# A fused transformer sandwich on one core: weighted sums in two pieces, the first batch's splits on other engines, later loads issued later

## The reference

```python
c_kv = x @ W_kv_down
k_rope = _rotary_apply(c_kv @ W_k_rope, cos, sin)
k = (c_kv @ W_k_up).reshape(Bb, Tt, NH, HD)          # NH = 16 heads, HD = 16
v = (c_kv @ W_v_up).reshape(Bb, Tt, NH, HD)
q = (x @ W_q).reshape(Bb, Tt, NH, HD)
q_rope = _rotary_apply(x @ W_q_rope, cos, sin)
scores = jnp.einsum('bqhd,bkhd->bhqk', q, k)
scores = scores + jnp.einsum('bqr,bkr->bqk', q_rope, k_rope)[:, None]
scores = scores / math.sqrt(HD + D_R)
scores = jnp.where(causal[None, None], -jnp.inf, scores)
w = jax.nn.softmax(scores, axis=-1)
attn = jnp.einsum('bhqk,bkhd->bqhd', w, v).reshape(Bb, Tt, D_MODEL)
return attn @ W_o
```

## Time and profile before

| | |
|---|---|
| median of 3 runs | 1363.53 us (1363.21 to 1367.56) |
| the profiled execution | 1369.83 us, span 1368.0 us |
| PE busy | 1197.1 us, 88% |
| DVE busy | 1114.6 us, 81% |
| ACT busy | 1057.5 us, 77% |
| POOL busy | 258.2 us, 19% |
| mean granted TensorE clock | 0.945 |
| weighted sums on PE (L982) | 2560 records, 93.3 us busy |
| turns of the weights on PE (L964) | 1280 records, 201.0 us busy |
| copies of the turned weights on ACT (L1217) | 300, 172.1 us busy |

### The profile page before, as it was taken

One profiled execution on the slowest core, in us unless ns is written; L12 is line 12 of the kernel. 1 busy time (PEld: TensorE's weight loads), 2 busy tenths in 40 slices (PEclk: granted clock), 3 DMA queues, 4 the chain that ended last, 5 costly groups with the idle time before them and its releaser, 6 DMA issues.

```text
span 1368.0 us, 23221 instructions
## 1 busy us (share of the span) xinstructions
PE 1197.1 (88%) x8060; PEld 774.9 (57%) x8060; DVE 1114.6 (81%) x2323; ACT 1057.5 (77%) x2113; POOL 258.2 (19%) x253
## 2 busy tenths in 40 slices
PE   5898985989899899998899999999999998973867
PEld 2574754466555655665655755676565764641434
DVE  3693588898689988999899998899889997799930
ACT  4675799768979989798868989698968987548542
POOL 3952001300121103200131010400131111111011
PEclk9799997999999999999999999999899998995979
DMA  8412350424134115311452131612342131013000
GB/s 256 107 23 73 59 147 26 111 44 126 40 80 98 24 47 159 85 30 32 134 121 57 25 103 46 147 23 59 107 106 58 24 119 39 31 56 100 16 16 16
DMA packets 72083, 101.64 MB, mean 74 GB/s; under 512 B 10640, under 2 KB 44064, under 8 KB 71968
## 3 DMA queue, kind: packets, MB, share of 16 engines
q1 hardware_dynamic: 71968, 100.16, 27.9%
HBM read 74.44 MB, written 25.69 MB: 73 GB/s over the span
## 4 chain that ended last, share of the span: by engine, by line
PE 51%; ACT 20%; DVE 17%; issue 8%; DMA 2%; POOL 1%; SPq 0%; POOLq 0%; DVEq 0%; ACTq 0%
PE ps L881 21%; PE ps L890 13%; DVE work L1526 6%; ACT work L1210 4%; PE ps L964 4%; PE ps L982 3%; DVE work L1445 3%; ACT work L1217 3%; ACT xnd L1153 3%; PE ps L956 3%; PE ps L1050 2%; DVE work L1535 1%; PE ps L873 1%; DVE work L1400 1%; ACT work L1276 1%
## 5 line engine op out<-in xcount | busy, mean ns | idle before, releaser
L1526 DVE TENSOR_TENSOR_SCAN work<-work 128x512 f32<-128x512 f32 x256 | 305.3, 1223 | 31.1 <-ACT work L1276 29.1
L1210 ACT ACTIVATE work<-work 128x384 f32<-128x384 f32 (+3 forms) x512 | 265.8, 564 | 42.5 <-DVE work L1445 41.6
L763 POOL TENSOR_TENSOR later_norms<-later_norms,singles 128x2 f32<-128x2 f32 x112 | 101.6, 910 | 884.0 <-ACT xnd L1153 577.0
L1445 DVE CUSTOM_DVE_ANT_0 work<-ps,work 128x384 f32<-128x384 f32 (+3 forms) x512 | 224.2, 485 | 48.1 <-PE ps L956 44.9
L964 PE MATMUL ps<-ident,work 128*128 128x128 f32 x1280 | 201.0, 282 | 25.0 <-ACT work L1210 23.2
L964 PEld LDWEIGHTS ps<-ident,work 128*128 128x128 f32 x1280 | 151.4, 145 | 75.2 <-issue 52.1
L1217 ACT COPY work<-ps 128x512 f32<-128x512 f32 x300 | 172.1, 579 | 3.9 <-PE ps L964 3.7
L1535 DVE TENSOR_TENSOR work<-work 128x1024 f32<-128x1024 f32 x128 | 161.9, 1265 | 5.1
L956 PE MATMUL ps<-work 96*128 96x384 bf16 (+3 forms) x512 | 123.7, 310 | 10.6 <-DMA work<-scratch 5.2
L881 PE MATMUL ps<-led_xTd,wf 128*128 128x512 f32 x256 | 124.7, 635 | 6.7 <-issue 6.0
L890 PE MATMUL ps<-wf,hid 128*128 128x256 f32 x512 | 116.9, 389 | 4.4 <-ACT hid L1292 3.6
(11 more groups left out here) (177 smaller groups left out, 1919.6 us busy)
## 6 DMA issues: line engine op xcount, KB each, us to landing
work<-values SPq DMA_DIRECT2D x64, 256.0 KB, 3.2
work<-ratios SPq DMA_DIRECT2D x64, 256.0 KB, 3.3
scratch<-work SPq DMA_DIRECT2D x32, 384.0 KB, 4.8
work<-scratch SPq DMA_DIRECT2D x64, 192.0 KB, 3.9
work<-scratch SPq DMA_DIRECT2D x64, 128.0 KB, 4.2
x_in<-x SPq DMA_DIRECT2D x8, 512.0 KB, 6.5
work<-scratch SPq DMA_DIRECT2D x64, 64.0 KB, 4.2
values<-work SPq DMA_DIRECT2D x16, 256.0 KB, 2.7
```

The costliest lines, as they stand in the source:

```text
L763: g_.tensor_tensor(rstds[chain][:, tokens], spreads[chain][:, tokens], power[:, tokens], ALU.pow).then_inc(*rstd.one)
L1210: i = s_.activation(part_of, part_of, ACT.Exp, scale=-1.0, bias=nmax[:, row:row + 1])
L1445: i = v_.tensor_tensor_reduce(sc[:, n % 4, at:at + nk], out_of(b, name)[:, at:at + nk], base_of(qt), -SCORE_SCALE, BIG, ALU.add, ALU.min, ...
L1526: v_.tensor_tensor_scan(ring[:, at, m, :], pwr[:, slot, :], ring[:, at, m, :], 0.0, ALU.mult, ALU.add).then_inc(*scanned.one)
```

## The change

The second and the third piece of a group's weighted sums become one. The list of items keeps the lag of five units, so a group has a piece after units 3 and 9, of 32 and 48 records. Units 4 to 7 are thus held in their slots until the last piece. In batch 0 a new item "cast" has ACT cast the rest and DVE subtract, in place of POOL. The twelve later loads go to a function that SP calls in batch 0 after the load of group 1. `MERGE` and `BANKS` are new for all engines.

```diff
-SUMS = ((3,), (2, 0), (1,))
-SUM_OF = (0, 0, 0, 0, 1, 1, 1, 1, 2, 2)
-SUM_AFTER = (3, 7, 9)
+SUMS = ((3,), (2, 0, 1))
+SUM_OF = (0, 0, 0, 0, 1, 1, 1, 1, 1, 1)
+SUM_AFTER = (3, 9)
...
-    items = ["ckv", ("q", 0), ("q", 1), ("pieces", 0), "qr", ("k", 0), ("k", 1), ("pieces", 1), "kr", ("v", 0), ("v", 1),
+    items = ["ckv", ("q", 0), ("cast", 0), ("q", 1), ("cast", 1), ("pieces", 0), "qr", ("k", 0), ("cast", 2), ("k", 1), ("cast", 3),
+             ("pieces", 1), "kr", ("v", 0), ("v", 1),
...
+            def load_rest():
+                load(raw_re, w_in_re)
...
+                load(b2r[:], b2)
...
                     load_group(b, n)
+                    if b == 0 and n == 1:
+                        load_rest()
...
-                if item in ("q", "k"):
+                if item in ("q", "k") and b:
...
-                    need_given(pool, second_piece)
+                    need(pool, second_piece, b, n + 1 + DC * (item == "k"))
...
-                    for m in range(last - 1 if k == 2 else last - 3, last + 1):
+                    for m in range(hg * UNITS + (SUM_AFTER[k - 1] + 1 if k else 0), last + 1):
...
+                if item == "cast" and b == 0:
+                    name, piece = (f"k{n - DC}", k_pieces[:, n - DC, 1, :]) if n >= DC else (f"q{n}", q_pieces[:, n, 1, :])
+                    is_drained(act, b, name)
+                    s_.copy(piece, rest[:, n % DC, :]).then_inc(*second_piece.one)
...
+                if item == "cast" and b == 0:
+                    pieces, pick = (q_pieces, (1, 2)) if n < DC else (k_pieces, (1, 0))
+                    need(dve, second_piece, b, n + 1)
+                    v_.tensor_tensor(pieces[:, n % DC, pick[1], :], rest[:, n % DC, :], pieces[:, n % DC, pick[0], :],
+                                     ALU.subtract).then_inc(*third_piece.one)
```

More of the change, by code:

```diff
@@ L164 @@
     "pe": "xT ckv q qr k kr v base S T PV OT attnT out fxT fc fproj zxT z total query gather oout gxT gc gproj prep",
-    "act": "ystats fstats fystats zstats oystats gstats gystats centre norm xT q k v S T PV attnT fnorm fxT fc znorm zxT z weights query turn fold cos sin silu gnorm gxT gc gsum ternary prep",
-    "dve": "stats ckv q qr k kr base S T OT sum fc fsum z weights ratio total rates turn frac scan mix gate silu "
+    "act": "ystats fstats fystats zstats oystats gstats gystats centre norm xT q cast k v S T PV attnT fnorm fxT fc znorm zxT z weights query turn fold cos sin silu gnorm gxT gc gsum ternary prep",
+    "dve": "stats ckv q cast qr k kr base S T OT sum fc fsum z weights ratio total rates turn frac scan mix gate silu "
            "osum gystats ternary prep tables means late",
@@ L174 @@
     "pe":
[9 rows of a table removed]
-    "act":
[14 rows of a table removed]
-    "dve":
[13 rows of a table removed]
[10 rows of a table added]
+    "act":
[15 rows of a table added]
+    "dve":
[13 rows of a table added]
     "pool":
-        "a2 p a3 p4 a4 d2 a3 d7 a4 d2 a3 d8 a4 d2 a3 d8 a d3 a d a5 d10 a d4 a6 d10 a d4 a3 d2 a3 d9 a d3 a6 d14 "
+        "a p5 a9 d2 a2 d7 a4 d2 a3 d8 a4 d2 a3 d8 a d2 a d a2 d a3 d10 a d4 a6 d12 a d2 a3 d2 a3 d8 a d4 a6 d14 "
         "a2 d26 p4",
     "sp":
-        "a14 d3 m4 d m4 d m9 a6 d2 a m4 d3 m10 a5 m d m2 d a2 d3 m4 d2 m9 a5 m2 d m2 d a2 d3 m4 d m4 d m5 a3 m a2 "
-        "m3 d2 a2 d2 m4 d2 m2 d m9 a3 m a2 m d2 a2 d3 m4 d m5 d m5 a5 m2 d m d a2 d3 m4 d m4 d m8 d m d3 m4 d3 "
-        "m13 d4",
+        "a14 d2 m4 d3 m13 a6 d4 m8 a d m6 a2 m a2 m a d m d a2 d3 m8 d2 m5 a5 m3 d m d a2 d2 m4 d2 m4 d m5 a3 m "
+        "a2 m2 d m d a2 d3 m3 d m5 d m6 a m a2 m a m a d2 a2 d2 m4 d2 m4 d m6 a2 m a3 m2 d2 a2 d2 m4 d3 m13 d5 m8 "
+        "d2 m9 d4",
@@ L229 @@
-3057613054762130547630215476305274163052741630542163054635321403765410642504136205436104275316471256
-4157261750623716520753012752073157235163720561326372406137024561374537025370621475036217241750267502
-4130567412564273015231706253716231540716520462745206742657014271064214710245172035470157263140652316
-7346521730517462305167240516705162405716240573425321067451046145304261534605421730652714637256473256
-4357042364507560276250763125703624135067215473507214536074574261305742613507261350267350216340572163
@@ L234 @@
-4507123013675210372607514306712546170256172065137305216372130710235170423150726140375624705647123056
-413702564137256413072564132056432170564317052643170526431705
+0123450123450134250134250314203512405241024512045320145203420352043251042531025412504125014325140321
+4351234051230541236705412367054123670541236754261375240356472365743025461725364213451046120356471023
+6547130267406342670146032574163702416350241356024135062731406273106542731062437104265732531326735132
+7543743256731463243701426734120746573201456215702456017426315670216403721675640356213547021354217503
@@ new lines @@
+4175203471526340156423654356535637015743176025137016234763127640216705164720531425170315047130651453
+6502163502714635027143560271437561403275614027561402756210453726413762346075340265742360157362045607
+5214720425107234105274307520472542043765124735604172305471302654371243605712436057214367021436702143
+6720451367041652370162756736012534017542073415073104357041732013427105347031765304751364052317064530
+4251634205716305427105632710275106325710634572016534706231057214051026475120637146530173421073524705
@@ L236 @@
+4372650426351472654215762401725643075124630174236701453702614325670143256701325670312670354267512704
+3615024657102674510652073156247035074653763074356145136041501340574153450724157364015237165237401652
+703164527031452703614527034652374016523701652437016524370165
 """
@@ L656, in load_group @@
                     at += k * HD
+            def load_rest():
+                load(raw_re, w_in_re)
+                load(raw_im, w_in_im)
+                load(fac, factors)
+                load(dist, c_dist)
+                load(sel[:], c_sel)
+                load(carry[:], c_carry)
+                load(wz[:], w_in_val)
+                load(wzs[:], w_in_dec)
+                load(wout[:], w_out)
+                load(wf1[:], w1.rearrange("(c p) n -> p c n", p=P))
+                load(wf2[:], w2.rearrange("(c p) n -> p c n", p=P))
+                load(b2r[:], b2)
             load_x(0)
@@ L679, in _ @@
             raw(raw_v[0:RANK], v)
-            load(raw_re, w_in_re)
-            load(raw_im, w_in_im)
-            load(fac, factors)
-            load(dist, c_dist)
-            load(sel[:], c_sel)
-            load(carry[:], c_carry)
-            load(wz[:], w_in_val)
-            load(wzs[:], w_in_dec)
-            load(wout[:], w_out)
-            load(wf1[:], w1.rearrange("(c p) n -> p c n", p=P))
-            load(wf2[:], w2.rearrange("(c p) n -> p c n", p=P))
-            load(b2r[:], b2)
             def do(b, item, n):
```

5 lines of the change are left out of this document (removed), and 74 rows, old and new, of the table MERGE.

## The result

The changed kernel takes 1374.69 us (median of 10 runs, 1369.29 to 1376.82), the kernel before 1364.04 in the same session (ten runs too, one of them at 2056.49, which the median passes over): a ratio of 1.0072, 95% interval 1.0059 to 1.0086. It is slower by some 10 us, where 3 us less had been forecast; the range ended at 1372. A second set of runs gave 1375.07 and 1.0076 (1.0056 to 1.0096).

What follows compares the result with a forecast made beforehand. PE was taken to set the pace in the middle, the first score's delay to pass on in the first batch. Start 3.3 plus tail 0.6 less pieces 7.0 gave −3.1: median 1360.4 us, range 1351 to 1372.

Steps and rivals of the forecast that it cites:

- the pieces' gain: Weighted sums in two pieces: 5.8 us of saved entries and 5.7 of PE waits, 10.8 at most; two thirds taken, 7.0.
- The new wait: ACT's copy of unit 10 waits for the joined piece: 0.05 us a group, counted as nothing, upper end 1.5 a group.
- rival (b): Copy of unit 10 does wait, ACT's exponentials slip, PE waits three units later: +11.9, 1375.4 us; chance 0.13.
- Rival (a): Pieces gain nothing, since ACT and DVE set the pace and PE's freed time idles: +3.9, 1367.4 us; chance 0.17.
- The start: First batch, splits by ACT and DVE: first score 4.0 us later, at 49.1; first batch ends 3.3 later.
- rival (d): POOL's ternary work, slowed by DVE's subtractions, holds DVE at prep 4 until 50.1: 0.8 over forecast, 1361.2 us; chance 0.08.
- Loads put off: Twelve later weight loads moved behind the second group's load: cost nothing, 2 us if the margin is gone.
- The tail: Copy of query 2 ahead of ACT's turns and one addition ahead of the last product: 0.6 us lost (0 to 1.2).
- Past the first batch the lists keep their neighbours: Rewritten lists of all engines keep the same neighbours within a few units past the first batch.
- seams: Other places where the rewritten lists differ: 3 us either way in the range, nothing in the sum.

Runs made afterwards that it cites:

- p2: Kernel before with its own orders, first batch and splits; only the middle piece of the sums joined with the last: 1385.28 us, ratio 1.0152.
- ml_hold: mid_last_c with one wait more: the middle piece also waits for the copies of units 8 and 9; 1377.62 us, ratio 1.0097.
- ml_release: mid_last_c with one wait longer: copies of units 10 to 13 wait for the last piece, not the middle one; 1370.99 us, ratio 1.0055.
- after_ml: Changed kernel with the joined piece split in two again, the middle one directly ahead of the last at the same place: 1369.15 us, ratio 1.0035.
- mid_last_c: Kernel before, three pieces, the middle one moved directly ahead of the last in all 32 groups, nothing else moved: 1366.41 us, ratio 1.0014.
- a3: Changed kernel, its first batch and orders, with three pieces, the middle one back behind the transposes of unit 9: 1402.16 us, ratio 1.0269.
- x_ahead: Kernel before's orders and three pieces behind the changed kernel's first batch, loads put off included: 1369.32 us, ratio 1.0038.
- mid_last: Kernel before, middle piece moved directly ahead of the last in the chain's list, which also shifted other items on PE and ACT: 1401.84 us.
- mid_next_c: Kernel before, three pieces, PE's middle piece one score and one set of transposes later in groups 0 to 2, nothing else moved: 1366.08 us, ratio 1.0005.
- p2_early_c: p2 with the joined piece and ACT's copy of its sums one score and one set of transposes earlier in groups 0 to 2: 1402.76 us, ratio 1.0274.

## Why the prediction was wrong

Two steps failed: the wait that was put at 0.05 us a group and so at nothing, and the two thirds of the pieces' gain that were counted as time.

**The new wait** was 0 in the sum and costs 5 to 6 us. The prediction let the joined piece end where the last one ended, 0.24 earlier, and got 0.05 us of waiting a group. That holds for PE's work but not for its inputs. Without M, PE comes to ML 1.26 earlier, at 933.39 in the earlier trace rows (an estimate: the transposes of unit 11 then wait for ACT's exponential, which ends at 932.69, and from about 0.15 behind that they hold PE for 0.54). ACT's copy of unit 9 does not come earlier; here it is in the kernel before, a row that the prediction did not look at:

```profile
933.67 0.58 ACT L1217 COPY work<-ps 128x512 f32<-128x512 f32 x1
```

It ends at 934.25. So PE waits 0.9, ML starts 0.15 later as in p2 and, 1.54 long, ends at about 935.9, and the copy of unit 10, which came at 935.01, waits 0.9. p2 has 0.94 and 1.07 there. In before, M filled that time. By ml_hold, ml_release and p2 the two waits cost 11 and 6 us, 19 together, in the old orders, and 5 to 6 in the changed kernel's own (after_ml). The sign of rival (b), ACT's copies waiting for PE's sums by over 7 us, is there with 11.4. It named ACT's side of it and came nearest with 1375.4, but for half the reason: PE's side was missing, and its sum left the pieces a gain of 4. That it hit the number is luck in part. The prediction named 1.5 us a group as the upper end of this wait and then left it out of the range.

**The pieces' gain** was right in size and wrong in effect: 7.0 in the sum, nothing in the time. The saved entry is there (6.2 us less busy in mid_last_c, forecast 5.8), the waits before M are there (5.0, forecast 5.7), and 48 matmuls take 1.54 as forecast. "Two thirds are taken" should have read "none, net": mid_last_c, which has the whole gain and of the two waits only 4.4 us of ACT's, is at 1.0014, and its interval (0.9996) leaves room for about half a microsecond of the 11. How much was never on the path, and how much ACT's 4.4 us gave back, is not separated. Rival (a) was right here. That PE is busy for 94% of the middle was no ground for a share. Nor does "none" hold for every order: between a3 and after_ml the same two terms, 7.5 and 18.9 us, go with 33 us of time. after_ml stands as far over before as the changed first batch alone (1.0035 and 1.0038), so what its new orders and the pieces bring comes to nothing together.
The Trainium skill, "TensorEngine Tiling (Array Packing)", section Tiling Modes, has TensorE drain when the tiling mode changes; the trace agrees with a price: PE's list has 89 entries into these matmuls in before and 64 in mid_last_c, and 6.2 us for 25 entries less is 0.25 each (forecast 0.24), which did not become time there. The prediction counted 24 entries, since it took eight last groups to have the two pieces back to back; it is seven.

**The start** went as forecast up to the first score: the raw loads landed at 20.15 (forecast 20.2), the last cast is at 34.51 (35), the first score at 48.85 (49.1; 47.68 in the second profile). Then rival (d) came true as well. POOL was done at 49.75, not 48.4, and DVE stood at prep 4 until 49.89 (50.1 by (d)), so the first score was taken 4.8 us later than before, the 4.0 + 0.8 of that rival. In the second profile it was taken 3.55 later. Three of POOL's instructions beside DVE's work:

```profile
29.48 1.47 POOL L835 TENSOR_SCALAR work<-work 128x256 f32<-128x256 f32 x1
...
33.37 1.61 POOL L836 TENSOR_SCALAR work<-work 128x256 f32<-128x256 f32 x1
...
37.38 1.74 POOL L835 TENSOR_SCALAR work<-work 128x256 f32<-128x256 f32 x1
```

The others of this kind take 1.22 to 1.24. The end of the batch moved by 2.3 to 3.2 (forecast 3.3), the end of the kernel by 5.2 (x_ahead). What adds the last 2 us, behind the first batch, is not settled.

**The other terms.** Loads put off: forecast at nothing, and not tried alone; in x_ahead their price cannot be told from that of the casts. The tail: 0.3 (0.6). "Past the first batch the lists keep their neighbours": false in effect. The orders differ little to the eye, yet the choice of M's place, early or late, is worth 33 us in the new ones (a3, after_ml) and nothing that can be told in the old (before, mid_last_c).

**The sum as it is now**: the start 5, the join's waits 5 to 6, its gain nothing: 10 to 11, measured 9.8 (ratio) and 10.6 (medians). Against the forecast of -3.1 that is 7 for the gain, 5 to 6 for the wait and 2 for the start. The forecast's own range was also drawn too narrow: its terms (start 0.8 to 4.5, tail 0 to 1.2, pieces -10.8 to -3, seams 3 either way) add up to 1350.5 to 1369.2, not 1352 to 1367. No version ran faster than the kernel before.

## What to carry to other kernels

When two pieces of work are merged, the merged one starts when its latest input is there and frees its buffers when its last part is done: check both against the other engines' rows at that place, not only the sum of the durations. The piece that was ready early was what the engine did while it waited; its overhead (about 0.25 us an entry) was cheaper than the idle time it covered. In a fixed merge of several queues, move one item at a time with all others held in place, or the run measures the shift of the rest (mid_last 1401.84, mid_last_c 1366.41). And price a move in the orders in which it will run: the same move of M was worth nothing in one set of orders and 33 us in another.

## What the runs showed of the hardware

POOL's two-scalar operation on 128x256 float32 took 1.22 us alone. It took 1.47 and 1.61 beside DVE's subtractions of two tensors at 29.16 and 33.19 (0.69 each), and 1.74 beside DVE's addition of the rotary part at 37.39 (0.71). At 35.16 it was the other way round: POOL's kept its 1.22 and this subtraction took 0.89:

```profile
35.16 0.89 DVE L1435 TENSOR_TENSOR work<-xna,work 128x512 bf16<-128x512 f32 x1 [0.68 <-ACT work L1206]
```

So one of the two loses 0.2 to 0.5 us. At 29.16 and 33.19 DVE had begun first (POOL at 29.48 and 33.37) and POOL lost; at 35.16 POOL had begun first, at 34.96, and DVE lost; at 37.38 the two began within 0.01 us and POOL lost. The Trainium skill, "GPSIMD Engine Reference", section Specifications, has the two share an SBUF interface when DVE reads two SBUF inputs; the trace agrees that they hinder each other, by less than the length of DVE's instruction.

An entry from the transposes into the 32-column matmuls and out of them again cost PE 0.25 us by 25 entries less (before, mid_last_c) and 0.26 by 29 (a3, after_ml). These are differences of busy times with modelled ends, and rough: mid_next_c has 91.4 us with 89 entries, p2_early_c 91.7 with 64. Taking 25 of them out of 1364 us did not show in the time of mid_last_c.
